# Last stage of a 4096-token block on one core: GpSimd takes the rounded rows of x between the two tiles of h, and the layer norms' Newton step moves from VectorE to GpSimd

## The reference, cut to what matters

```python
def fp4_quant_dequant(x):                       # blocks of 16 along the last dim
    scale = jnp.maximum(jnp.max(jnp.abs(xb), axis=-1, keepdims=True) / 6.0, 1e-12)
    idx = jnp.searchsorted(_MID, jnp.abs(xb / scale))
    return (_GRID[idx] * jnp.sign(xb / scale) * scale).reshape(shape)

gate = fp4_linear(x, w_gate)                    # 256 -> 704
y = fp4_linear(x, w_up)                         # 256 -> 704
h = jax.nn.silu(gate) * y
return fp4_linear(h, w_down)                    # 704 -> 256
...
x = x + _layernorm(_L1_attn_ref(...))           # norm 0: of y; its sum is x3
x = x + _layernorm(_L1_ffn_ref(_layernorm(x)))  # norm 1: of x3, norm 2: of the output
```

## Time and profile before

| what | value |
|---|---|
| median of 3 runs | 3698.08 us (3696.91 to 3700.52) |
| the profiled execution, its own time | 3687.84 us |
| its span in the profile | 3686.1 us |
| mean granted TensorE clock | 0.932 |
| busy over the span: PE / DVE / ACT / POOL | 3230.1 / 2950.5 / 2059.5 / 1196.9 us |
| last stage, from 3236 us to 3686 us of the span: PE / DVE / ACT / POOL busy | 330.5 / 349.4 / 205.1 / 286.1 us of 450 |

### The profile page before, as it was taken

One profiled execution on the slowest core, in us unless ns is written; L12 is line 12 of the kernel. 1 busy time (PEld: TensorE's weight loads), 2 busy tenths in 40 slices (PEclk: granted clock), 3 DMA queues, 4 the chain that ended last, 5 costly groups with the idle time before them and its releaser, 6 DMA issues. The chain is left out here.

```text
span 3686.1 us, 87940 instructions
## 1 busy us (share of the span) xinstructions
PE 3230.1 (88%) x34874; PEld 1852.7 (50%) x34875; DVE 2950.5 (80%) x4783; ACT 2059.5 (56%) x2972; POOL 1196.9 (32%) x974
## 2 busy tenths in 40 slices
PE   4889999999999999984999765997799999967876
PEld 1543333333333333344666542343677787746665
DVE  5778999999999999925566354776699999948986
ACT  0316777777777777762011155665565757434553
POOL 0310000000000000006011370000899999927775
PEclk8868999999999999996999877998899999989998
DMA  1552112020202020035222353333544434231110
GB/s 57 194 151 24 21 29 45 5 45 5 46 10 58 20 56 6 5 115 203 82 65 65 112 168 124 119 119 128 150 127 122 136 106 134 78 120 52 57 34 18
DMA packets 223121, 296.00 MB, mean 80 GB/s; under 512 B 72872, under 2 KB 159536, under 8 KB 220592
## 3 DMA queue, kind: packets, MB, share of 16 engines
q1 hardware_dynamic: 209872, 261.98, 25.0%
q0 software_dynamic: 6144, 17.05, 1.4%
q10 hardware_dynamic: 6752, 11.96, 0.9%
HBM read 174.35 MB, written 115.95 MB: 79 GB/s over the span
## 5 line engine op out<-in xcount | busy, mean ns | idle before, releaser
L999 DVE TENSOR_REDUCE att_maxima<-att_ps_m 128x1 f32<-128x512 f32 x2048 | 1285.6, 684 | 66.6 <-PE att_ps_m L1055 65.1
L954 ACT ACTIVATE att_probs<-att_ps_s 128x1024 f32<-128x1024 f32 x1024 | 999.7, 1022 | 282.7 <-PE att_ps_o L1084 269.8
L1084 PE MATMUL att_ps_o<-att_probs,held_vs 128*32 128x256 f32 x8192 | 658.8, 393 | 4.9 <-ACT att_probs L954 0.6
L2426 POOL TENSOR_TENSOR ss_ch<-ss_h,ss_c_rep 128x1024 f32<-128x1024 f32 x256 | 602.2, 2439 | 9.4 <-DVE ss_h L2513 9.4
L1055 PE MATMUL att_ps_m<-held_ks,held_qs 48*128 48x512 f32 x2048 | 585.1, 512 | 14.0 <-PEq L60 13.4
L2545 PE MATMUL ss_ps_u<-ss_diag,ss_dx_t 128*32 128x128 f32 x16384 | 473.4, 274 | 29.5 <-DMA ss_dx_t<-scratch_dx_t 16.0
L2545 PEld LDWEIGHTS ss_ps_u<-ss_diag,ss_dx_t 128*32 128x32 f32 x16384 | 452.6, 111 | 85.7 <-issue 69.0
L1055 PEld LDWEIGHTS att_ps_m<-held_ks,held_qs 48*128 48x128 f32 x2048 | 238.3, 188 | 458.1 <-DVE att_maxima L999 392.4
L1070 PE MATMUL att_ps_s<-held_qs,held_ks 50*128 50x512 f32 x2048 | 454.7, 405 | 2.8 <-ACT att_probs L954 0.8
L2465 ACT ACTIVATE ss_decay<-ss_delta,ss_a_neg 128x1024 f32<-128x1024 f32 x256 | 293.8, 1148 | 228.6 <-DVE ss_h L2513 205.9
L1084 PEld LDWEIGHTS att_ps_o<-att_probs,held_vs 128*32 128x32 f32 x8192 | 162.7, 108 | 362.5 <-issue 341.3
(11 more groups left out here) (394 smaller groups left out, 4469.1 us busy)
## 6 DMA issues: line engine op xcount, KB each, us to landing
ss_delta<-scratch_delta SPq DMA_DIRECT2D x256, 128.0 KB, 3.1
held_qs<-scratch_q SPq DMA_DIRECT2D x96, 128.0 KB, 4.6
held_ks<-scratch_k SPq DMA_DIRECT2D x96, 128.0 KB, 4.9
ex_x<-scratch_sorted_x SPq DMA_DIRECT2D x72, 132.0 KB, 2.0
scratch_sorted_y<-ex_y SPq DMA_DIRECT2D x72, 128.0 KB, 1.7
scratch_q<-held_parts SPq DMA_DIRECT2D x16, 512.0 KB, 4.6
scratch_k<-held_parts SPq DMA_DIRECT2D x16, 512.0 KB, 5.5
moe_w_w<-in_W SPq DMA_DIRECT2D x16, 512.0 KB
```

Of the source, the lines that this page charges most:

```text
L954: act.activation(probs[:, (2 * n + pair) % 4, :, :], ps_s[pair][:, :, :], ACT.Exp, scale=HD ** -0.5).then_inc(exp_done, 1)
L999: dve.tensor_reduce(maxima[:, j, at:at + 1], ps_m[plan.bank(key)][:, :], AX.X, ALU.max).then_inc(maxed, 1)
L1084: mm = pe.matmul(ps_o[h * VW:(h + 1) * VW, cols], vs[st // QC % 2][:, kt, h * VW:(h + 1) * VW], probs[:, (2 * n + h // 2) % 4, h % 2, cols ...
L2426: pool.tensor_tensor(ch[:, w.n % (CH_GROUPS * DQ), :], h[:, w.n % H_SLOTS, :], c_rep[:, w.ng, :], ALU.mult).then_inc(s["ch_ready"], 1)
```

## The change

Four things change, all inside `fp4_ffn`.

- The Newton step, `scales`, leaves DVE. On POOL it is seven instructions instead of four, since POOL is given only tensor_tensor and tensor_scalar: two that prepare `var_eps` and `mean_neg`, and a chain of five, with a semaphore wait ahead of each of the last four. It stands with number -1, so POOL's step s does the scales of step s + 1, between the rows of h and `times_up`.
- `scale_h` keeps only the subtractions. The multiplications into `hq` become `place_h`, one tile at a time, and `scale_x` stands between the two tiles. `hq_ready` now counts tiles, and PE's `turn_h` waits for its own tile.
- POOL's steps are unrolled, so its waits are on constants.
- DVE's `variances` first waits for `scale_ready` of the step before, since POOL reads `moments`.

```diff
-                def scales(step, parity):
-                    c = Chain(dve, s["rstd_steps"], step * NEWTON)
-                    dve.wait_ge(s["rstd_ready"], step + 1)
-                    c.then(dve.scalar_tensor_tensor(newton[:, :], r0[:, :], -0.5, r0[:, :], ALU.mult, ALU.mult))
...
-                run_stages(dve, UNITS4, (stats_out, 6), (add_xm, 0), (stats_x3, 1), (variances, 0, STEPS4), (split_xq, 2), (scales, 0, STEPS4),
+                run_stages(dve, UNITS4, (stats_out, 6), (add_xm, 0), (stats_x3, 1), (variances, 0, STEPS4), (split_xq, 2),
                            (make_h, 4), (make_x3, 0), (make_x, 1), (make_out, 6), unroll=True)
...
                 def variances(step, parity):
+                    dve.wait_ge(s["scale_ready"], step)
...
+                def place_h(u, slot, k):
+                    if k == 0:
+                        pool.wait_ge(s["hq_turned"], u * UT * 2)
+                    for i, f in enumerate(halves(FFN)):
+                        pool.wait_ge(s["hq_steps"], (u * UT + k) * 2 + i + 1)
+                        at, n = k * HB // UT + f.start // FP4, FFN // 2 // FP4
+                        ins = pool.tensor_tensor(in_blocks(hq[:, k, f]), in_blocks(h_round[:, k, f]),
+                                                 over(h_scale[:, at:at + n].unsqueeze(2), [P, n, FP4]), ALU.mult)
                     ins.then_inc(s["hq_ready"], 1)
...
+                def scales(step, parity):
+                    pool.wait_ge(s["var_ready"], (step + 1) * NT)
+                    for n, behind in enumerate(BEHIND):
+                        done = min(max(step - behind, 0), UNITS4)
+                        pool.wait_ge(s[("z_ready", "xf_ready", "o_taken")[n]], done * UT)
+                    c = Chain(pool, s["rstd_steps"], step * SCALES)
+                    c.then(pool.tensor_scalar(var_eps[:, :], var, EPS, None, ALU.add))
+                    c.then(pool.tensor_scalar(mean_neg[:, :], mean, -1.0, None, ALU.mult))
+                    pool.wait_ge(s["rstd_ready"], step + 1)
+                    c.then(pool.tensor_tensor(newton[:, :], r0[:, :], r0[:, :], ALU.mult))
+                    c.wait()
+                    c.then(pool.tensor_tensor(newton[:, :], var_eps[:, :], newton[:, :], ALU.mult))
+                    c.wait()
+                    c.then(pool.tensor_scalar(newton[:, :], newton[:, :], -0.5, 1.5, ALU.mult, ALU.add))
+                    c.wait()
+                    c.then(pool.tensor_tensor(rstd[:, :], newton[:, :], r0[:, :], ALU.mult))
+                    c.wait()
+                    pool.tensor_tensor(nmr[:, :], mean_neg[:, :], rstd[:, :], ALU.mult).then_inc(s["scale_ready"], 1)
...
-                run_stages(pool, UNITS4, (times_sigmoid, 3), (scale_h, 4), (scale_x, 1), (times_up, 2))
+                run_stages(pool, UNITS4, (times_sigmoid, 3), (scale_h, 4), (first_tile(place_h), 4), (scale_x, 1), (second_tile(place_h), 4),
+                           (scales, -1, STEPS4), (times_up, 2), unroll=True)
...
-                    pe.wait_ge(s["hq_ready"], u + 1)
+                    pe.wait_ge(s["hq_ready"], u * UT + k + 1)
```

More of the change, by code:

```diff
@@ L2683, in fp4_ffn @@
         eps = r.sb("ln_eps", [P, 1])
-        lnv, r0, newton, rstd, nmr = (r.sb("ln_" + n, [P, NT]) for n in ("lnv", "r0", "newton", "rstd", "nmr"))
+        lnv, r0, newton, rstd, mean_neg, var_eps, nmr = (r.sb("ln_" + n, [P, NT]) for n in ("lnv", "r0", "newton", "rstd", "mean_neg", "var_eps", "nmr"))
         mean, var = (moments[:, :, i:i + 1].rearrange("p n o -> p (n o)") for i in range(2))
@@ L2687, in fp4_ffn @@
         ps_gu, ps_h = r.ps("ps_gu", [P, 3, GN]), r.ps("ps_h", [P, 2 * GT, P])
-        names = ("padded", "rstd_steps", "z_steps", "x_steps", "o_steps", "h_steps", "q_steps", "var_ready", "ln_ready", "rstd_ready",
+        names = ("padded", "rstd_steps",  "z_steps", "x_steps", "o_steps", "h_steps", "q_steps", "var_ready", "ln_ready", "rstd_ready",
                  "proj_ready", "proj_taken", "x3_ready", "xq_ready", "xq_turned", "xq_high", "xq_low", "gu_ready", "gu_taken", "gu_used",
@@ L2723, in _ @@
                 dve.wait_ge(s["padded"], 3)
-                NEWTON = 3
                 def stats(n, x, k):
@@ L2789, in make_h @@
                     x, m, q = blocks_of(h[:, slot, :, :]), blocks_of(h_magic[:, :, :]), blocks_of(h_round[:, :, :])
-                    dve.wait_ge(s["hq_ready"], u)
+                    dve.wait_ge(s["hq_ready"], u * UT)
                     fp4_scale(dve, c, x, h_amax[:, :], h_scale[:, :], h_inv[:, :])
@@ L2840, in scale_h @@
                             pool.tensor_tensor(h_round[:, k, f], h_round[:, k, f], h_magic[:, k, f], ALU.subtract).then_inc(s["hq_steps"], 1)
[L2841 to L2847, removed]
@@ new lines, in first_tile, with second_tile @@
+                def first_tile(stage):
+                    return lambda u, slot: stage(u, slot, 0)
+                def second_tile(stage):
+                    return lambda u, slot: stage(u, slot, 1)
+                SCALES = 6
+                def scales(step, parity):
[16 more added lines that the diff above has]
+                    pool.tensor_tensor(nmr[:, :], mean_neg[:, :], rstd[:, :], ALU.mult).then_inc(s["scale_ready"], 1)
+                    assert c.n == SCALES, c.n
```

## The result

The changed kernel takes 3721.14 us (median of 6 runs, 3719.55 to 3726.58), the kernel before 3698.86 us (6 runs, 3696.91 to 3701.52): ratio 1.005 on record, 95% interval 1.0029 to 1.007. It is slower by 0.5%, and the interval leaves out 1.

The account below looks back on a forecast made before the run. It took mutual exclusion of VectorE's passes and GpSimd's instructions as the weightier bound. Twelve steps +12 us, start +1.6 and end +3.4 made +17 on 3687.8 us; with 10.2 us to the median, 3715 us, range 3680 to 3731.

Parts of the forecast that it names:

- Newton step on GpSimd, 1.9 us: Last stage, GpSimd: seven instructions at 0.17 us and four waits on itself at 0.19 us add 1.9 us a step.
- Cover lost, 4.3 us: Last stage: VectorE's four passes over h, until now in GpSimd's idle time, meet its multiplications and cost it 4.3 us.
- Passes over h of 2.4, 1.6, 1.6 and 2.4 us: Sign of being right: VectorE's four passes over h lengthen to these from 1.62, 0.89, 0.90 and 1.63 us.
- faster: Rival: late x and Newton step were the bound, passes over h bear company; 3674 us, chance 0.17 in two forms.
- x before the second tile of h: GpSimd's order in a step: it could start on x 6.7 us after `h_rounded` instead of 8.6.
- VectorE's wait at the split gone: VectorE's wait of 1.20 us a step for x at the split should go, a sign of being right.
- GpSimd's sum of 24.7 us decides, VectorE has 23.9: Length of a step: the larger engine sum sets it, 24.7 us, 1.0 us longer than before.
- Twelve steps +12 us, start +1.6, end +3.4, in all +17: Last stage: time added in its twelve overlapped steps, its first two steps and its last norms, +17 us together.
- weaker form: Rival: only one-operand VectorE passes exclude GpSimd's instructions; GpSimd 21.8 us a step, about 3680 us, within the shared chance 0.17.
- Much slower: Rival: GpSimd's Newton chain lands on the passes over h; 26.5 us a step or more, about 3735 us, chance 0.08.
- The unrolling: Experiments' rival: the price is that of GpSimd's unrolled steps; the prediction gave unrolling nothing; no chance stated.
- the exchanged order: Experiments' rival: the price is that of GpSimd taking x between the tiles of h; no chance stated.

Follow-up runs that it names:

- after_reduce: Changed kernel with the first and last VectorE pass over h replaced by block maxima, leaving out the rounding of h: 3686.55 us, ratio 0.9963.
- swap_only: Changed kernel with the Newton step back on VectorE, keeping x between the two tiles of h and the unrolled steps: 3698.54 us, ratio 0.9987.
- swap_merge: Changed kernel with the Newton step back on VectorE and GpSimd's subtractions over h and x in fewer, longer instructions: 3696.8 us, ratio 0.9983.
- the two last kernels: after_merge_sub and after_merge_all, the changed kernel with fewer, longer GpSimd instructions: ratios 1.004 and 1.0061.
- after_merge_sub: Changed kernel with GpSimd's subtractions merged, two of 704 columns over h for four, one of 512 over x for two: ratio 1.004.
- after_merge_all: Changed kernel with GpSimd's subtractions, multiplications and placing of h in one 704-column instruction per tile, and one subtraction over x: ratio 1.0061.
- after_extra4: Changed kernel with four more six-column GpSimd instructions ahead of the Newton step, into a tile nobody reads: 3732.86 us, ratio 1.0083.
- unroll_only: Kernel before with nothing changed but GpSimd's steps unrolled: 3702.73 us, ratio 0.9999.
- before_reduce: Kernel before with the first and last VectorE pass over h replaced by block maxima, leaving out the rounding of h: 3701.63 us, ratio 0.9996.
- newton_only: Changed kernel with both tiles of h ahead of x again, the Newton step staying on GpSimd: 3737.07 us, ratio 1.0087.

## Why the prediction was right

It was right in sign and size, and in the mechanism that it gave most weight, the lost cover of the passes over h. Two things in it were wrong, the end of VectorE's wait at the split and the rule that GpSimd's sum alone decides; and the close number owes something to luck, since errors in the Newton price cancelled. Its terms against the traces, per step where nothing else is said:

- *Newton step on GpSimd, 1.9 us* (7 x 0.17 and 4 x 0.19): 1.9 us from first to last. The two halves were off and cancelled: an instruction takes 0.20 to 0.25 us, a wait on itself leaves a gap of only 0.08 us. The estimate of 0.07 us for six columns, which I drew from the figures of the Trainium skill ("GPSIMD Engine Reference", section 3.1), is contradicted by 0.20 us; the page itself gives no figure for so few columns.
- *Cover lost, 4.3 us*: the multiplications of h are 51.7 us longer over twelve steps, 4.3 us a step. after_reduce shows that it hangs on the passes over h. GpSimd's other instructions over h and x are 0.2 us a step shorter, and its waits at the Newton step (for the statistics and for ScalarE's guess) add 0.3.
- *Passes over h of 2.4, 1.6, 1.6 and 2.4 us*: means of 1.89, 1.52, 1.51 and 2.24. The first one gets in without a wait in some steps (1.63 us in the step shown), and GpSimd's multiplication then waits for it (2.39 us instead of 0.92). So the sign by which the prediction would have let the rival "faster" win, a first pass of 1.6 us while GpSimd works, was seen and did not mean that: it takes GpSimd's side to tell.
- *x before the second tile of h, reached 6.7 us after `h_rounded`*: 6.35 us, from 3534.22 to 3540.57 us. *VectorE's wait at the split gone*: wrong. It is 16.8 us in twelve steps, where it was 16.0. The exchanged order alone takes it to 5.0 us (swap_only); with the Newton step on GpSimd as well, GpSimd has no idle time left ahead of `h_rounded`, takes it up later, and the lead is gone again. That last link is read from the tables, not tested. The wait is 4 to 6 us in after_reduce, where GpSimd is free sooner, and in swap_merge and the two last kernels, where VectorE comes to the split late itself.
- *GpSimd's sum of 24.7 us decides, VectorE has 23.9*: 24.6 us a step, so the number held. That the larger sum decides was wrong. GpSimd is busy for 23.7 us, VectorE for 22.2 with its waits inside, and each lengthens the other: shortening GpSimd alone (after_merge_sub, after_merge_all) did not shorten the step, and lengthening it (after_extra4) moved it by 0.5 of 0.8 us. I take it that the work of the pair decides, and how finely it is cut; the runs fit that, but none of them varies it alone.
- *Twelve steps +12 us, start +1.6, end +3.4, in all +17*: 10.7, 3.2 and 3.5, in all 17.4 us. The start is not clear of its scatter: unroll_only and before_reduce, as fast as the kernel before, have 86.4 and 90.1 us there against its 89.0. The end is 70.7 to 71.5 us wherever the Newton step is on VectorE, and 74.8 us and more where it is on GpSimd, but 70.8 in after_reduce: so the last passes over h have a part in it, for which I had given nothing, and 3.5 us for my 3.4 is partly luck. The 3715 us stood 6 us below the measured 3721; the 17 us lie within the 11 to 26.
- *The rivals*: "faster" fell by the row of 2.24 us for a two-operand pass that ran beside GpSimd, and by GpSimd's longer multiplications. Its weaker form held that only the one-operand passes exclude; after_reduce took out the two-operand ones alone and gave back 2.45 us a step. The section of the Trainium skill that the prediction leans on ("Advanced Engine Details and Errata", "VectorE Performance Modes") names only the two-port kind as blocked by GpSimd, but the same page under "GPSIMD Details" names VectorE instructions with two SBUF inputs as well. These runs agree with the wider form: both kinds of pass are lengthened. "Much slower" had about the time of newton_only (25.9 us a step, 1.0087), but not its mechanism: there the chain waits for ScalarE's guess and lands on no pass (its instructions take 0.20 to 0.25 us); in the changed kernel the second tile of h between the statistics and the Newton step keeps it from that wait. "The unrolling" and "the exchanged order" cost nothing.

## What to carry to other kernels

The engines were said at the outset to meet only through semaphores; VectorE and GpSimd also meet instruction by instruction, and nothing in a kernel's text shows it. GpSimd's idle time may be the cover of the very VectorE passes that it can't run beside: look which passes lie in it before giving GpSimd more work, and price each pass that loses the cover at nearly its whole length, on GpSimd. Busy time of such a pair holds waiting, so moving 2.5 us of small instructions from one to the other, or merging instructions on one side, need not be a gain; here neither was. A short chain that hangs on a third engine wants other work between its input and itself, as here the second tile of h.

## What the runs showed of the hardware

- VectorE and GpSimd hand over instruction by instruction: a one-operand pass of 1408 columns takes 0.89, 1.52 or 2.25 us beside an idle GpSimd, instructions of 352 columns (0.92 us) and of 704 (1.67 us). Seen from GpSimd, one of 352 columns that starts 0.04 us behind a pass of 1.63 us takes 2.39 us.
- Block maxima and statistics are not lengthened in any kernel here: `fp_h_amax` takes 1.61 us, beside whatever GpSimd did. Nor is the two-operand split of x, one of whose operands lies in PSUM (0.66 to 0.69 us).
- A GpSimd instruction of six columns takes 0.20 us, and 0.24 to 0.25 us where it reads the moments, of which it takes every other element; a product of two full operands takes 0.92 us for 352 columns and 1.67 us for 704 at the least: one in place of two saves 0.17 us.
- The same code ahead of the last stage takes up to 25 us more or less from one execution and chip to the next (3236 to 3261 us here), more than the change is worth: compare stages, not spans.
